# A two-layer attention, expert and recurrent kernel on one core: one chain for the experts' sum, a new order on every engine, and the last sums on TensorE

## The chip, the core and the metric

The kernel runs on one core of a Trainium2 chip. The metric is the device time of one execution in microseconds; the slowest core counts, and here there is one.

## What is computed

The input x has 128 sequences of 64 rows and 128 features, that is 8192 rows or 64 tiles of 128 rows; the context has the same shape. Four blocks follow each other, each with a residual:

```python
x = x + L0_xattn(layernorm(x), ctx, ctx)   # 16 heads of 8, biases, 64 queries against 64 keys of the same sequence
x = x + L0_ffn(layernorm(x))               # 8 experts, the two best by a gate
x = x + L1_xattn(layernorm(x), ctx, ctx)   # 16 heads, no biases
x = x + L1_ffn(layernorm(x))               # a recurrence over the 128 sequences

# the experts: every expert is computed, w is zero for those not chosen
scores = xf @ W_gate + b_gate
w = one_hot(top_k(scores, 2)) weighted by the two scores
out = sum_e w[:, e] * (relu(xf @ W1[e] + b1[e]) @ W2[e] + b2[e])

# the recurrence: one cell state of (64, 128), 128 steps, its end added to every row
ft = sigmoid(xt @ wf.T + c @ uf.T + bf); it = sigmoid(...); gt = tanh(...)
c = ft * c + it * gt
h = tanh(x @ wo.T + c_final @ uo.T + bo)
```

The last line needs the final state, so nothing of the output can be finished before the last of the 128 steps.

## The kernel before

All of x and ctx stays in SBUF (tiles `x` and `cx`, 64 tiles of 128 x 128). A software pipeline written out in full runs over iterations i from FIRST to LAST. In iteration j of the normalisation the four blocks work on different tiles: the first on tile j, the experts on tile j - L1, the second attention on tile j - L2, the recurrence on tile j - L3. Each small step is a Python function, and the table `LAG` says how many iterations after its tile's turn a step stands. Each engine's loop calls its functions in a fixed order, written by hand; engines meet through semaphores (`sig(name)`), one for each step, and wait for counts. With L3 = 10 there are 74 turns of x, 54 of which carry all four blocks; the others, at both ends, carry fewer.

PSUM has seven banks in rotation (`banks[0:7]`) and one, `lstm`, for the recurrence. `USES` lists the 23 uses of an iteration in TensorE's order, and who reads each. A use takes the next bank, so TensorE waits until the reader of the use seven places ahead is done (function `bank`). The readers S0 to S3 of the scores are VectorE's differences D0 to D3.

What the steps are called in the profile:

- `x` to `xn` (L596, ScalarE) is the normalisation; it needs `rs` and `mr` (L1076, L1078, GpSimd), which need VectorE's `mv`, `nm`, `ve` (L813 to L817, function `spread`). `xn` is turned by TensorE (L301) and copied to `xT` by ScalarE (L583, once an iteration).
- Scores (L334), their maxima `mx` (L827, VectorE, four an iteration) and differences to `Ex` (L841, four), exponentials (L625, ScalarE), turns (L349) and copies `ET` (L636), values (L379), halves of the row sums `h` (L1092 and L1096, GpSimd, two pairs an iteration), sums `sm` (L852) and reciprocals (L863), `aT` (L875), the projection (L395), its addition to x (L888).
- The experts: `sc`, `top`, `tix`, `tif` (L899 to L920), the two weights `wa` and `wb` (L931), their sum `we` (L943), its bf16 pieces `wep` (L1123 to L1129, GpSimd), hidden layers (L418), outputs y0 and y1 in two banks (L439), and in `combine` eight SCALAR_TENSOR_TENSOR (L961), which add the weighted outputs in two chains: `acc0` starts from x, `acc1` from the experts' bias, which ScalarE copied from PSUM (L699). L965 adds the two chains into x.
- The recurrence: products (L486), gates (L717 to L719, ScalarE), then `AB` (L975) and `CG` (L978, VectorE), twice an iteration (functions `update(i, 0)` and `update(i, 1)`); two SBUF inputs each.
- `Km` (L1049) and `Vb` (L1063), GpSimd, spread keys and values; L1106 adds the bias of the first attention to x.

```python
                        e.scalar_tensor_tensor(d, b[:, 128 * n:128 * n + 128], we[:, s, k:k + 1],
                                               d if n or c else x[:, t, :], ALU.mult, ALU.add).then_inc(sig(f"acc{c}"), 1)
```

At the end `cU` (L1030) is the last state's part of the output, and `finish` adds it to `cx`, which by now holds x @ wo.T, in chunks of 512 columns (L1166), ScalarE takes the tanh (L765), and the same engine adds the chunk to x (L1172) for SP to store. `TAIL` gives 44 tiles to VectorE and 20 to GpSimd.

Of the kernel before, what the change touches and what calls it, by code (L numbers as in the profile page):

```python
# [7 lines left out]
P = 128  # L8
NT = 64
# [27 lines left out]
L1, L2, L3 = 4, 6, 10  # L37
LAG = {"kv": 0, "sB": 2, "S": 1, "xin": 1, "h0": 1, "h1": 1, "e0": 2, "pv": 3, "sA": 1, "rt": 3,
# [7 lines left out]
OFF = (0, L1, L2, L3)  # L46
FIRST, LAST = -1, NT + 12
# [6 lines left out]
USES = [("kv", "kvc", 0, "C", 1), ("S0", "D0", 1, "A", 1), ("S1", "D1", 1, "A", 1),  # L54
# [10 lines left out]
def on(t):  # L65
    return 0 <= t < NT


def build(nc, a, const, out):
    ctx = ExitStack()  # L70
    with ctx:
# [70 lines left out]
        acc = sb("acc", [P, 2, 2, 128])  # L142
# [36 lines left out]
        def sync_program(e):  # L179
# [42 lines left out]
            lo, done = 0, {"dve": 0, "pool": 0}  # L222
            for adder, n in TAIL:
                done[adder] += 1
                e.wait_ge(sig("out_" + adder), done[adder])
                e.dma_start(o_v[:, lo:lo + n, :], x[:, lo:lo + n, :]).then_inc(sig("stored"), 16)
                lo += n
# [4 lines left out]
        def tensor_program(e):  # L232
            def bank(i, name, done=()):
# [258 lines left out]
            for i in range(FIRST, LAST):  # L492
                if i == FIRST + 1:
                    project_bias()
                if FIRST + 2 <= i < FIRST + 5:
                    turn_weights(i - FIRST - 1)
                keys_values(i)
                step(i, 1)
                scores(i)
                cell_inputs(i)  # L500
                hidden(i, 0)
                hidden(i, 1)
                turn_e(i, 0)
                values(i)
                step(i, 0)
                turn_r(i)
                turn_x(i)
# [728 lines left out]
```

## Time and profile before

| | |
|---|---|
| median of 3 runs | 980.34 us (980.33 to 986.9) |
| profiled execution | 981.66 us, of which the span of the trace is 979.7 |
| busy share of the span | TensorE 88%, VectorE 86%, ScalarE 84%, GpSimd 63% |
| TensorE's granted clock, mean | 0.964 |
| chain that ended last | VectorE 60%, TensorE 20%, no visible cause 12%, ScalarE 3% |

Busy times are means over ramps and steady iterations, so a time for one iteration is better read from two starts of the same instruction, one iteration apart. The spans of neighbouring instructions overlap by some 0.08 us: what an instruction takes from its engine is the distance from its start to the next start, not its own length.

### The profile page before, as it was taken

What the parts mean: (1) busy time and instruction counts of PE and PEld (TensorE: products, weight loads), DVE (VectorE), ACT (ScalarE), POOL (GpSimd) and SP (SyncE); (2) the same over time, 40 slices, a digit from 0 to 9 for tenths busy, and PEclk for the clock granted to TensorE, in tenths of its full rate; (3) what the DMA queues carried; (4) which work ended last, traced back from release to release, by engine and by line L of the source; (5) the groups of instructions that cost most, each with busy time, mean ns of one, the idle gap of its engine ahead of it and who ended that gap; (6) DMA issues with size and microseconds to landing.
All of it is one profiled execution on the core that took longest, in us unless ns stands there. A gap on an engine that the chain in (4) does not pass through costs nothing.

```text
span 979.7 us, 37648 instructions
## 1 busy us (share of the span) xinstructions
PE 859.3 (88%) x13267; PEld 763.5 (78%) x13267; DVE 843.1 (86%) x2878; ACT 820.0 (84%) x2650; POOL 618.8 (63%) x1026
## 2 busy tenths in 40 slices
PE   2778889999999999999999999999999999988750
PEld 1467778888888888888888888888888888877540
DVE  0377899999999999999999999999999999988638
ACT  2467789999999999999999999999999999877633
POOL 2455666676766676766676766676766676754415
PEclk9689999999999999999999999999999999999975
DMA  6920000000000000000000000000000000000006
GB/s 134 250 58 2 2 3 3 3 4 3 2 3 3 3 3 3 3 3 3 3 3 3 2 3 3 3 3 3 3 3 2 4 3 3 3 2 2 2 1 171
DMA packets 37991, 17.34 MB, mean 18 GB/s; under 512 B 9176, under 2 KB 37792, under 8 KB 37808
## 3 DMA queue, kind: packets, MB, share of 16 engines
q1 hardware_dynamic: 37248, 14.67, 5.9%
q8 instruction: 110, 1.80, 0.8%
q14 instruction: 73, 0.60, 0.2%
q0 software_dynamic: 128, 0.07, 0.1%
q10 hardware_dynamic: 432, 0.21, 0.1%
HBM read 10.74 MB, written 4.19 MB: 15 GB/s over the span
## 4 chain that ended last, share of the span: by engine, by line
DVE 60%; PE 20%; issue 12%; ACT 3%; SPq 2%; DVEq 1%; POOL 1%; DMA 0%; ACTq 0%; POOLq 0%
DVE acc L961 13%; DVE mx L827 11%; DVE Ex L841 11%; PE ps L395 4%; PE ps L349 3%; DVE x L965 3%; PE ps L360 3%; PE ps L301 3%; DVE AB L975 3%; DVE x L888 2%; DVE mv L813 2%; PE ps L439 2%; DVE st L786 2%; DVE CG L978 2%; PE ps L461 2%
## 5 line engine op out<-in xcount | busy, mean ns | idle before, releaser
L1092 POOL TENSOR_TENSOR h<-Ex 128x512 f32<-128x512 f32 (+1 forms) x140 | 165.6, 1183 | 155.0 <-issue 135.8
L827 DVE TENSOR_REDUCE mx<-ps 128x8 f32<-128x512 f32 (+1 forms) x280 | 166.1, 635 | 30.5 <-PE ps L334 30.5
L636 ACT ACTIVATE ET<-ps 128x512 f32<-128x512 f32 (+1 forms) x280 | 160.5, 573 | 10.3 <-PE ps L349 10.0
L841 DVE TENSOR_TENSOR Ex<-ps,mx 128x512 f32<-128x512 f32 (+1 forms) x280 | 165.6, 630 | 0.0
L349 PE MATMUL ps<-cst,Ex 128*128 128x128 f32 x1024 | 150.1, 276 | 4.8 <-ACT kv L564 2.1
L625 ACT ACTIVATE Ex<-Ex 128x512 f32<-128x512 f32 (+1 forms) x280 | 152.5, 611 | 0.0
L1076 POOL TENSOR_TENSOR rs<-ve,half 128x4 f32<-128x4 f32 (+3 forms) x74 | 69.1, 934 | 119.9 <-DVE ve L817 119.9
L677 ACT ACTIVATE hT<-ps,col 128x128 f32<-128x128 f32 x512 | 137.2, 371 | 0.0
L439 PE MATMUL ps<-w,hT 128*128 128x128 f32 x1024 | 131.6, 283 | 0.0
L349 PEld LDWEIGHTS ps<-cst,Ex 128*128 128x128 f32 x1024 | 119.3, 143 | 9.6 <-ACT kv L564 4.4
L418 PE MATMUL ps<-xT,w 128*128 128x128 f32 x1024 | 125.4, 276 | 0.0
L439 PEld LDWEIGHTS ps<-w,hT 128*128 128x128 f32 x1024 | 122.5, 196 | 0.0
L418 PEld LDWEIGHTS ps<-xT,w 128*128 128x128 f32 x1024 | 119.5, 192 | 2.3 <-issue 2.3
L961 DVE SCALAR_TENSOR_TENSOR acc<-ps,we,acc 128x128 f32<-128x128 f32 x448 | 121.1, 342 | 0.1
L596 ACT ACTIVATE xn<-x,mr,rs 128x128 f32<-128x128 f32 x256 | 106.1, 484 | 9.9 <-POOL mr L1078 9.5
L1096 POOL TENSOR_TENSOR h<-h 128x256 f32<-128x256 f32 (+1 forms) x140 | 96.3, 688 | 20.2 <-POOL h L1092 0.5
L379 PE MATMUL ps<-ET,Vb 128*32 128x64 f32 x4096 | 72.5, 222 | 25.7 <-DVE Ex L841 25.5
L379 PEld LDWEIGHTS ps<-ET,Vb 128*32 128x32 f32 x4096 | 61.1, 111 | 42.3 <-DVE Ex L841 41.9
L717 ACT ACTIVATE TG<-ps,col 128x64 f32<-128x64 f32 x128 | 39.5, 309 | 52.5 <-PE ps L486 52.5
L334 PE MATMUL ps<-Km,qT 32*64 32x256 f32 x2048 | 74.5, 394 | 7.1 <-DVE acc L961 7.0
L1049 POOL TENSOR_TENSOR Km<-kT,cst 128x512 f32<-128x512 f32 x64 | 66.5, 1040 | 21.4 <-ACT kT L554 21.4
L486 PE MATMUL ps<-CG,wT 128*64 128x64 f32 x1536 | 71.5, 230 | 3.3 <-DVE CG L978 3.3
(111 smaller groups left out, 1951.2 us busy)
## 6 DMA issues: line engine op xcount, KB each, us to landing
out_dram<-x SPq DMA_DIRECT2D x15, 256.0 KB, 2.5
x<-in_x_dram SPq DMA_DIRECT2D x7, 512.0 KB, 7.0
cx<-in_ctx_dram SPq DMA_DIRECT2D x7, 512.0 KB, 6.8
w<-in_L_ffn_W_dram SPq DMA_DIRECT2D x2, 512.0 KB, 5.1
x<-in_x_dram SPq DMA_DIRECT2D x1, 256.0 KB, 3.0
cx<-in_ctx_dram SPq DMA_DIRECT2D x1, 256.0 KB, 3.3
out_dram<-x SPq DMA_DIRECT2D x2, 128.0 KB, 2.2
b<-in_L_ffn_b_dram SPq DMA_DIRECT2D x9, 4.0 KB
```

The source lines that it names most:

```text
L349: m = e.transpose(b[:, 128 * n:128 * n + 128], Ex[:, j % 2, r, 128 * n:128 * n + 128], ident)
L379: m = e.matmul(b[32 * r:32 * r + 32, 128 * c + 64 * n:128 * c + 64 * n + 64], Vb[:, c, j % 4, n, r, 2 * w:2 * w + 2, :].rearrange("p a c - ...
L418: m = e.matmul(b[:, 128 * n:128 * n + 128], w1[:, 4 * c + n, :], xT[:, (t + L1) % 2, 1, :], start=True, stop=True, skip_group_check=True)
L439: m = e.matmul(b[:, 128 * n:128 * n + 128], hT[:, t % 2, 4 * c + n, :], w2[:, 4 * c + n, :], start=True, stop=True, skip_group_check=True)
L596: m = e.activation(xn[:, s, k, :], x[:, j - OFF[k], :], ACT.Identity, bias=mr[:, s, k:k + 1], scale=rs[:, s, k:k + 1])
L625: e.activation(Er, Er, ACT.Exp, scale=SCALE).then_inc(sig(f"E{r}"), 1)
L636: e.activation(ET[:, j % 2, r, lo:hi, :, :], b[:, 256 * lo:256 * hi].rearrange("p (c w q) -> p c w q", c=hi - lo, w=2), ACT.Copy).then_inc ...
L677: m = e.activation(hT[:, t % 2, k, :], b[:, 128 * n:128 * n + 128], ACT.Relu, bias=col[:, B1 + k:B1 + k + 1])
L827: e.tensor_reduce(mx[:, j % 2, r, 4 * lo:4 * hi], b[:, 256 * lo:256 * hi].rearrange("p (j k) -> p j k", k=64), AX.X, ALU.max).then_inc(sig ...
L841: e.tensor_tensor(Ex[:, j % 2, r, 256 * lo:256 * hi].rearrange("p (j k) -> p j k", k=64), b[:, 256 * lo:256 * hi].rearrange("p (j k) -> p ...
L961: e.scalar_tensor_tensor(d, b[:, 128 * n:128 * n + 128], we[:, s, k:k + 1], d if n or c else x[:, t, :], ALU.mult, ALU.add).then_inc(sig(f ...
L1092: e.tensor_tensor(u, v[:, :, :, 0:32], v[:, :, :, 32:64], ALU.add).then_inc(sig("half1"), 1)
```

## The change

The experts' sum becomes one chain: `combine(i, 0)` adds the bias bank to x (no copy by ScalarE), and `combine(i, 1)` to `combine(i, 8)` add the eight weighted outputs one after the other into one `acc`, the last one into x. The nine steps are called apart, so that others stand between some of them. `gate_sum` moves to GpSimd. All engines get a new order, `LAG` and `USES` are new, L1, L2, L3 are 5, 9, 14, and the loop has 81 iterations in place of 77, with 78 turns of x, 50 of them full. The turns of the later weights stand 4 iterations later. In the tail GpSimd has no part: for 30 tiles TensorE adds cU to cx by two products with the identity into a bank, from which ScalarE takes the tanh; for 34 tiles VectorE adds as before; VectorE alone adds the results to x.

```diff
-TAIL = [("dve", 4), ("pool", 4), ("dve", 4), ("dve", 4), ("pool", 4), ("dve", 4),
...
+TAIL = [("dve", 4), ("pe", 4)] * 7 + [("dve", 4), ("pe", 2), ("dve", 2)]
+EARLY = 2
-L1, L2, L3 = 4, 6, 10
+L1, L2, L3 = 5, 9, 14
-FIRST, LAST = -1, NT + 12
+FIRST, LAST = 0, NT + 17
...
-                if FIRST + 2 <= i < FIRST + 5:
-                    turn_weights(i - FIRST - 1)
+                if FIRST + 6 <= i < FIRST + 9:
+                    turn_weights(i - FIRST - 5)
...
+            def share(k, part):
+                lo, n = mine[k]
+                src = cx[:, lo:lo + n, :] if part == 0 else cU[:, :].unsqueeze(1).to_broadcast([P, n, 128])
+                return e.matmul(banks[k % 7][:, 0:128 * n], ident, src, start=(part == 0), stop=(part == 1),
+                                skip_group_check=True)
...
+                if n == 0:
+                    b = bank_of("yb", t + L1)
+                    e.wait_ge(sig("yb"), t + 1)
+                    e.tensor_tensor(d, b[:, 0:128], x[:, t, :], ALU.add).then_inc(sig("acc"), 1)
+                    return
+                c, k = (n - 1) // 4, (n - 1) % 4
+                b = bank_of(f"y{c}", t + L1)
+                if k == 0:
+                    e.wait_ge(sig(f"y{c}"), t + 1)
+                    e.wait_ge(sig("we"), t + 1)
+                e.wait_ge(sig("acc"), 8 * t + n)
+                m = e.scalar_tensor_tensor(x[:, t, :] if n == 8 else d, b[:, 128 * k:128 * k + 128],
+                                           we[:, t % 2, n - 1:n], d, ALU.mult, ALU.add)
...
+                e.tensor_tensor(we[:, s, :], wa[:, s, :], wb[:, s, :], ALU.add).then_inc(sig("we"), 1)
```

VectorE before, in a full iteration, from the last of the gate's weights over the experts' sum to the recurrence's second update and the maxima:

```order
L931 SCALAR_TENSOR_TENSOR wb<-cst,tif,top 128x8
L961 SCALAR_TENSOR_TENSOR acc<-ps,we,x 128x128
L961 SCALAR_TENSOR_TENSOR acc<-ps,we,acc 128x128 x7
L965 SCALAR_TENSOR_TENSOR x<-acc 128x128
L794 BN_STATS st<-x 128x6
L863 RECIPROCAL ri<-sm 128x32
L813 BN_AGGR mv<-st 128x2 x4
L816 SCALAR_TENSOR_TENSOR nm<-mv,ones 128x4
L817 SCALAR_TENSOR_TENSOR ve<-mv,ones 128x4
L975 SCALAR_TENSOR_TENSOR AB<-TG,CG 128x128
L978 SCALAR_TENSOR_TENSOR CG<-AB 128x64
L827 TENSOR_REDUCE mx<-ps 128x8 x3
```

VectorE now, from `ve` (which GpSimd waits for) to the same update; L970 is the experts' chain, L981 and L984 are AB and CG:

```order
L833 SCALAR_TENSOR_TENSOR ve<-mv,ones 128x4
L970 SCALAR_TENSOR_TENSOR acc<-ps,we,acc 128x128 x2
L915 TENSOR_TENSOR sc<-ps,bg 128x8
L970 SCALAR_TENSOR_TENSOR acc<-ps,we,acc 128x128
L922 MAX top<-sc 128x8
L970 SCALAR_TENSOR_TENSOR acc<-ps,we,acc 128x128 x2
L929 MAX_INDEX tix<-top,sc 128x8
L970 SCALAR_TENSOR_TENSOR acc<-ps,we,acc 128x128 x2
L970 SCALAR_TENSOR_TENSOR x<-ps,we,acc 128x128
L843 TENSOR_REDUCE mx<-ps 128x8
L981 SCALAR_TENSOR_TENSOR AB<-TG,CG 128x128
L984 SCALAR_TENSOR_TENSOR CG<-AB 128x64
```

Before, the update followed `ve` at once; now the whole experts' chain and one maximum stand between them.

GpSimd before, one iteration from the `rs` that waits for `ve`:

```order
L1076 TENSOR_TENSOR rs<-ve,half 128x4
L1078 TENSOR_TENSOR mr<-nm,rs 128x4
L1092 TENSOR_TENSOR h<-Ex 128x512
L1096 TENSOR_TENSOR h<-h 128x256
L1063 TENSOR_TENSOR Vb<-kv,cst 128x8x16 x2
L1123 CAST wep<-we 128x24
```

GpSimd now, from the same `rs`:

```order
L1106 TENSOR_TENSOR rs<-ve,half 128x4
L1108 TENSOR_TENSOR mr<-nm,rs 128x4
L1093 TENSOR_TENSOR Vb<-kv,cst 128x8x16 x2
L1164 CAST wep<-we 128x24
L1166 TENSOR_TENSOR wer<-we,wep 128x8
L1168 CAST wep<-wer 128x24
L1170 TENSOR_TENSOR wep<-wer,wep 128x24
L1122 TENSOR_TENSOR h<-Ex 128x512
L1126 TENSOR_TENSOR h<-h 128x256
L1122 TENSOR_TENSOR h<-Ex 128x512
L1126 TENSOR_TENSOR h<-h 128x256
```

The values and the gate's pieces now stand ahead of the halves of the sums, and both pairs of halves follow each other.

## Rows read from the trace of the kernel before

**Rows 1.** Stretches: us, busy PE, PEld, DVE, ACT, POOL; clock, DMA share, GB/s.

```profile
0.00:134.30 134.30, 93.13 (x1068) 74.04 (x1069) 79.11 (x282) 80.15 (x258) 69.07 (x126) 0.89 0.34 82
134.30:855.50 721.20, 691.73 (x11155) 628.17 (x11153) 675.96 (x2317) 668.21 (x2147) 494.45 (x811) 1.00 0.01 3
855.50:952.80 97.30, 74.45 (x1050) 61.27 (x1048) 63.76 (x257) 61.85 (x228) 38.83 (x81) 0.94 0.01 2
```

**Rows 2.** Groups by line and form: busy us, mean ns, idle before.

```profile
L583 ACT ACTIVATE xT<-ps 128x512 f32<-128x512 f32 x54 | 32.2, 597 | 3.0
L439 PE MATMUL ps<-w,hT 128*128 128x128 f32 x1024 | 131.6, 283 | 0.0
```

**Rows 3.** Timeline of VectorE, a full iteration: start, length, idle before.

```profile
502.48 0.16 DVE L817 SCALAR_TENSOR_TENSOR ve<-mv,ones 128x4 f32<-128x4 f32 x1
502.55 0.28 DVE L975 SCALAR_TENSOR_TENSOR AB<-TG,CG 128x128 f32<-128x128 f32 x1
502.87 0.23 DVE L978 SCALAR_TENSOR_TENSOR CG<-AB 128x64 f32<-128x64 f32 x1
503.01 1.88 DVE L827 TENSOR_REDUCE mx<-ps 128x8 f32<-128x512 f32 x3
504.81 0.45 DVE L943 SCALAR_TENSOR_TENSOR we<-wa,wb 128x8 f32<-128x8 f32 x1
505.18 1.27 DVE L841 TENSOR_TENSOR Ex<-ps,mx 128x512 f32<-128x512 f32 x2
...
508.66 0.42 DVE L875 TENSOR_TENSOR aT<-ps,rT 128x256 f32<-128x256 f32 x1 [0.41 <-issue]
...
509.59 0.28 DVE L777 BATCH_NORM_STATS2 st<-x 128x6 f32<-128x128 f32 x1
509.95 0.42 DVE L888 TENSOR_TENSOR x<-ps,x 128x256 f32<-128x256 f32 x1
510.29 0.16 DVE L899 TENSOR_TENSOR sc<-ps,bg 128x8 f32<-128x8 f32 x1
...
510.84 0.47 DVE L786 BATCH_NORM_STATS2 st<-x 128x6 f32<-128x128 f32 x2
...
512.05 0.35 DVE L961 SCALAR_TENSOR_TENSOR acc<-ps,we,x 128x128 f32<-128x128 f32 x1
...
514.33 0.47 DVE L965 SCALAR_TENSOR_TENSOR x<-acc 128x128 f32<-128x128 f32 x1
...
515.82 0.16 DVE L817 SCALAR_TENSOR_TENSOR ve<-mv,ones 128x4 f32<-128x4 f32 x1
```

**Rows 4.** Timeline of GpSimd, the same iteration.

```profile
502.71 1.02 POOL L1076 TENSOR_TENSOR rs<-ve,half 128x4 f32<-128x4 f32 x1 [1.41 <-DVE ve L817]
...
503.96 1.27 POOL L1092 TENSOR_TENSOR h<-Ex 128x512 f32<-128x512 f32 x1
505.38 0.73 POOL L1096 TENSOR_TENSOR h<-h 128x256 f32<-128x256 f32 x1
506.07 0.82 POOL L1063 TENSOR_TENSOR Vb<-kv,cst 128x128 f32<-128x128 f32 x2
506.83 0.21 POOL L1123 CAST wep<-we 128x24 bf16<-128x24 f32 x1
...
507.85 1.04 POOL L1049 TENSOR_TENSOR Km<-kv,cst 128x512 f32<-128x512 f32 x1
```

**Rows 5.** Timeline of all engines, in the ramp down.

```profile
884.24 0.48 DVE L931 SCALAR_TENSOR_TENSOR wb<-cst,tif,top 128x8 f32<-128x8 f32 x1
884.24 0.45 POOL L1096 TENSOR_TENSOR h<-h 128x128 f32<-128x128 f32 x1
```

**Rows 6.** Waits, longest in total: us, times, longest.

```profile
PE ps L256 <- DMA wst<-in_L_ffn_ui_dram: 10.8, 1, 10.8
```

**Rows 7.** Timeline of VectorE in the tail.

```profile
952.79 2.36 DVE L1166 TENSOR_TENSOR cx<-cx,cU 128x512 f32<-128x512 f32 x2
...
963.42 0.68 DVE L1166 TENSOR_TENSOR cx<-cx,cU 128x512 f32<-128x512 f32 x1
```

More of the change, by code:

```diff
@@ L221, in sync_program @@
                 load_c(c)
[L222 to L225, printed above, removed]
+            lo = 0
+            for k, (_, n) in enumerate(TAIL):
+                e.wait_ge(sig("out"), k + 1)
                 e.dma_start(o_v[:, lo:lo + n, :], x[:, lo:lo + n, :]).then_inc(sig("stored"), 16)
@@ L237, in bank @@
                 while v >= len(USES) * FIRST:
-                    _, reader, lag, chain, times = USES[v % len(USES)]
+                    _, reader, lag, chain, step, first = USES[v % len(USES)]
                     n = v // len(USES) - lag - SPAN[chain][0]
@@ L241, in bank @@
                         if reader not in done:
-                            e.wait_ge(sig(reader), times * (n + 1))
+                            e.wait_ge(sig(reader), step * n + first)
                         break
@@ L494, in tensor_program @@
                     project_bias()
-                if FIRST + 2 <= i < FIRST + 5:
-                    turn_weights(i - FIRST - 1)
+                if FIRST + 6 <= i < FIRST + 9:
+                    turn_weights(i - FIRST - 5)
+                hidden(i, 0)
                 keys_values(i)
+                step(i, 0)
+                values(i)
+                query(i)
+                turn_e(i, 3)
+                turn_w(i)
+                turn_e(i, 1)
+                turn_x(i)
+                out_inputs(i)
+                project(i)
+                expert_bias(i)
+                experts(i, 0)
+                turn_e(i, 2)
+                turn_r(i)
+                gate(i)
+                ctx_turn(i)
+                experts(i, 1)
+                turn_e(i, 0)
                 step(i, 1)
                 scores(i)
+                hidden(i, 1)
                 cell_inputs(i)
[L501 to L507, printed above, removed]
-                turn_e(i, 2)
-                turn_w(i)
-                out_inputs(i)
-                project(i)
-                gate(i)
-                expert_bias(i)
-                experts(i, 1)
-                experts(i, 0)
-                ctx_turn(i)
-                query(i)
-                turn_e(i, 3)
-                turn_e(i, 1)
+            mine, lo = [], 0
+            for adder, n in TAIL:
+                if adder == "pe":
+                    mine.append((lo, n))
+                lo += n
+            def share(k, part):
[3 more added lines that the diff above has]
+                                skip_group_check=True)
+            for _, reader, _, chain, step, first in USES:
+                e.wait_ge(sig(reader), step * (SPAN[chain][1] - 1) + first)
+            for k in range(EARLY):
+                share(k, 0)
             e.wait_ge(sig("C"), 2 * NT + 1)
@@ L1030, in vector_program, with share @@
             e.tensor_tensor(cU[:, :], lstm[:, 384:512], bo1[:, :], ALU.add).then_inc(sig("cU"), 1)
-            finish(e, "dve")
+            e.wait_ge(sig("cU"), 1)
+            e.wait_ge(sig("xo"), NT)
+            lo = [sum(n for _, n in TAIL[:k]) for k in range(len(TAIL) + 1)]
+            mine = [k for k, (adder, _) in enumerate(TAIL) if adder == "dve"]
+            def share(k):
+                e.tensor_tensor(cx[:, lo[k]:lo[k + 1], :], cx[:, lo[k]:lo[k + 1], :],
+                                cU[:, :].unsqueeze(1).to_broadcast([P, lo[k + 1] - lo[k], 128]),
+                                ALU.add).then_inc(sig("pre_dve"), 1)
+            share(mine.pop(0))
+            share(mine.pop(0))
+            for k in range(len(TAIL)):
+                e.wait_ge(sig("tanh"), k + 1)
+                e.tensor_tensor(x[:, lo[k]:lo[k + 1], :], cx[:, lo[k]:lo[k + 1], :], x[:, lo[k]:lo[k + 1], :],
+                                ALU.add).then_inc(sig("out"), 1)
+                if mine and k % 2 == 0:
+                    share(mine.pop(0))
         def gpsimd_program(e):
```

187 lines of the change are left out of this document (79 added, 108 removed), and 29 rows, old and new, of tables (LAG, USES).

## The prediction

> **What bounds the kernel now.** I read the table of stretches first [rows 1]. The kernel has three parts: 134.3 us until the recurrence joins, 721.2 us in which the 54 turns of x with all four blocks run [rows 2], so 13.36 us each, and 97.3 us down to the last state; a tail of 26.9 us follows, from 952.8 to the end of the span at 979.7. In the full turns TensorE is busy 691.7 of 721.2 us, VectorE 676.0 and ScalarE 668.2: no engine can be 10% slower, and none alone is full. The chain of waits decides between them: 60% of it is VectorE. So I walked one iteration of VectorE, from `ve` to `ve`, 502.48 to 515.82, 13.34 us [rows 3]. Its only wait of note is 0.41 us ahead of `aT`. What a faster VectorE can give is the question, and TensorE's 691.7 / 54 = 12.8 us is near: its matmul ends are modelled and its waits inside are short, so I put its own limit at 12.6 to 12.8 us an iteration.
>
> **VectorE's work in a full iteration**, in starts to next starts [rows 3]:
> - out: `we` (L943), 504.81 to 505.18, 0.37, now GpSimd's;
> - out: the old sum. Eight L961 take 512.05 to 514.33, 2.28: seven at 0.26 and 0.46 for the last, whose successor waits for two results of VectorE itself. L965 takes its 0.47 and about 0.04 until its reader starts. Together 2.79;
> - out: `sc` to `tix` as a chain of small ones that wait for each other, 510.29 to 510.84, 0.55; in the new order they stand between members of the experts' chain and fill its gaps;
> - out, if the new order does what it can: the wait at `aT` (two differences at 0.60 from 506.98 would let it start at 508.18, it starts at 508.66, so 0.48), and 0.16 at 509.59, where the statistic needs 0.20 and x comes after 0.36;
> - in: nine steps of one chain. A step that waits for the one just ahead starts 0.03 after its end (AB is 0.28 long from 502.55, CG starts at 502.87), so 0.35 + 0.03 = 0.38 in place of 0.26. Steps 1 to 2, 2 to 3, 3 to 4, 6 to 7 and 7 to 8 cost 0.38 each: 1.90 (`sc` and `top` hide in two of them). Step 4 to 5 crosses to the other bank and has three waits: 0.46 like the last L961. Step 5 to 6 holds the index search: 0.26 + 0.15 = 0.41. The last is free of followers: 0.26. The first, with the bias, is half of L888's work: 0.21. Together 3.24;
> - in: `stats_attention` now follows the addition to x directly and waits for it, 0.12.
>
> 13.34 - 0.37 - 2.79 - 0.55 - 0.64 + 3.24 + 0.12 = 12.35 us. So the moved and merged work is worth about 0.35 us (0.37 + 2.79 + 0.55 - 3.24 - 0.12), the better order up to 0.64.
>
> ScalarE loses the bias copy, 0.16 us of its 12.4; GpSimd gains a 128 x 8 sum, 0.2 us on 494.5 / 54 = 9.2. Neither becomes the bound.
>
> **What the order brings in: the port.** L943 is a 128 x 8 instruction and yet takes 0.45 us [rows 3]; it ends at 505.26, just after GpSimd's `h` (503.96 + 1.27 = 505.23) [rows 4]. A VectorE instruction with two SBUF inputs does not run beside such a GpSimd instruction, it waits for its end. Two instructions asked at the same time in the ramp down, and GpSimd's goes first: `wb` takes 0.48 us, twice the 0.23 of the larger CG, [rows 5]. In the tail a 128 x 512 addition takes 2.36 / 2 = 1.18 us, and later 0.60 when GpSimd is quiet [rows 7]. The experts' chain reads PSUM and is not touched. AB and CG have two SBUF inputs each. Before, they stood behind `ve`, when GpSimd computed `rs`, and took 0.28 and 0.23.
>
> Now count both engines from the start of `ve`, the common point. GpSimd: `rs` starts at 0.23, the work behind it at 1.48 (503.96 - 502.48); two Vb take 0.76, the four pieces 1.02, so `h` (L1122) runs from 3.26 to 4.53 and the second half from 4.68 to 5.41 [rows 4]. VectorE: 0.07 + 1.90 + 0.46 + 0.41 + 0.26 + one maximum 0.60 = 3.70: AB asks in the middle of `h`. It gets in when `h` is done and ends at about 4.68; CG asks at 4.71, when the second half has just begun, and ends at 5.41 + 0.08 = 5.49. Undisturbed it would end at 3.70 + 0.32 + 0.23 = 4.25. That is 1.24 us an iteration, on VectorE's own stream, where nothing covers it: the next maximum and all four differences stand behind it, and behind those TensorE's banks for the values, the query and the turns. The distance from `ve` to AB holds no wait for a slower engine as far as I can find one (TensorE's y0, y1 and S0 would each be there 0.5 us or more early), so it repeats. It would have to be off by 0.9 us to either side to go away.
>
> 12.35 + 1.24 = 13.59 us an iteration. The bounds: 12.6 (no stall, TensorE's limit) and 13.9 (both updates, below).
>
> **The ramps.** Before, 54 of 74 turns were full; now 50 of 78. Work is only moved: VectorE's busy time up to the last state was 79.1 + 676.0 + 63.8 = 818.9 [rows 1]. It loses about 64 x 0.72 = 46 us of busy time (L943 and most of L965) and gains some 5 for three more turns in which the attention runs by halves: 778. The 50 full turns hold 50 x 11.8 = 590 of it, which leaves 188 for the ramps against 142.9. Before, ramps took 134.3 + 97.3, less the 10.8 us in which TensorE stood at the turn of the weights until the last of them had landed [rows 6], so 220.8, a fill of 0.65. The 10.8 us go: four iterations later all weights are there. At 0.65 the ramps take 290 us, at 0.72, with the looser lags, 261, at 0.60 313. I take 0.67, near the row: 280. The weights' turns themselves are the same work.
>
> **The tail.** VectorE now has 17 additions to x and 9 of cU with GpSimd quiet: 23 at 0.60 and 3 of half size at 0.34, 14.8 us. TensorE: one product of 128 columns costs 131.6 / 512 = 0.257 us (two records each) [rows 2], so 30 tiles twice are 15.4, less 2.0 done early, at the full clock. The ramp down has a granted clock of 0.94 [rows 1], and it falls towards its end, when the recurrence alone runs; at 1.2 GHz throughout, TensorE would need 27 us. With about 2.2 us before the first result and 2.5 for the last store I take 19.5 us against 26.9; bounds 18 and 30.
>
> **The sum.** 280 + 50 x 13.59 + 19.5 = 979 us of span, against 979.7. The profiled execution lies 1.9 above its span and 1.3 above the median of the runs, so 979.6: I forecast **980 us**. A measurement of this kernel can tell about 1% from no change. In terms: full turns 679.5 against 721.2, ramps 280 against 231.6, tail 19.5 against 26.9.
>
> **Rivals.**
> 1. CG wins the port. CG asks only 0.03 us after GpSimd's second half starts. If it came first, only AB waits, 0.70 us: 13.05 an iteration, 27 us less, 953. Against it: GpSimd won a tie [rows 5].
> 2. No stall: the chain is short or AB finds the port free, and TensorE's 12.75 is the bound: 280 + 637.5 + 19.5, 938 us. The chain would have to be cheap: with steps at 0.26 AB asks 0.8 us earlier, ahead of `h`. For it: nothing in the rows; the pair AB, CG speaks against. The Trainium skill, VectorE: DVE Perf Modes, section "The DRAIN you can't avoid", has it that the semaphore between VectorE instructions costs nothing extra. By that the single chain is as cheap as two, and this rival would be the forecast; the trace disagrees, 0.26 from start to start in alternation against 0.32 for the shorter AB with its reader behind it.
> 3. Slower: the other update is caught too. `gate_sum` starts on GpSimd when `wb` ends, and the addition of the bias to x (0.46 us) follows it; CG of `update(i, 0)` asks about 0.49 us after the start of `wb`, the addition starts at about 0.46. If GpSimd is first, CG waits 0.28 more: 13.87 an iteration, 994 us. It decides from 0.03 us. Ramps at a fill of 0.60 would add 33 to any case and end on the same side.
> 4. The tail gives nothing, since TensorE stays at 1.2 GHz: 990 us.
>
> **Chances.** The forecast (AB and CG of one update wait) 0.40, rival 1 0.15, rival 2 0.19, rival 3 0.24, rival 4 0.02. With the ramps' uncertainty the forecast is within 1% of the 980.3 in 0.29 of its 0.40, rival 3 slower by more in 0.19, rivals 1 and 2 are faster. Faster 0.40, same 0.35, slower 0.25. The range that leaves out no more than 2 in 10 goes from 942 (most of rival 2 left out) to 998.
>
> **What the profile after would show.** A constant distance of 13.5 to 13.7 us between two `ve`; L981 with a mean well over 0.28 and L984 over 0.23, in one of the two updates each; L970 with starts 0.38 apart; L256 without a wait for a DMA; ramps of 280 us together; tail additions at 0.60. Wrong I would be if L981 shows 0.28 throughout, or if VectorE shows waits for TensorE between `ve` and AB, which would shift the meeting with `h`.

## The result, and the profile after

The changed kernel takes **939.5 us** (median of 4 runs, 938.75 to 939.64) against 980.68 us (980.33 to 986.9); the ratio is 0.957, with a 95% interval of 0.953 to 0.961. The forecast was 980 us with a range from 942, so the time lies just below the range. The span of the trace is 937.7 us. The same table of stretches as [rows 1], cut where the four blocks run together and where `cU` starts; the columns are span, busy PE, PEld, DVE, ACT, POOL, then clock, DMA share and GB/s:

```profile
0.00:128.90 128.90, 112.10 (x1399) 90.48 (x1400) 104.23 (x381) 102.16 (x343) 90.00 (x173) 0.97 0.36 85
128.90:799.00 670.10, 646.94 (x10337) 579.58 (x10336) 651.23 (x2097) 611.34 (x1946) 472.04 (x801) 1.00 0.01 3
799.00:918.50 119.50, 104.93 (x1540) 85.59 (x1538) 94.42 (x359) 87.36 (x315) 62.37 (x126) 0.96 0.01 2
918.50:937.70 19.20, 11.43 (x28) 5.24 (x28) 15.28 (x27) 9.46 (x17) 0.00 (x0) 0.94 0.77 219
```

In the terms of the prediction:

| | before | forecast | after |
|---|---|---|---|
| full turns | 54 x 13.36 = 721.2 | 50 x 13.59 = 679.5 | 50 x 13.40 = 670.1 |
| ramps, up and down | 134.3 + 97.3 | 280 | 128.9 + 119.5 = 248.4 |
| tail, from `cU` | 26.9 | 19.5 | 19.2 |
| span | 979.7 | 979 | 937.7 |

(The tail of before counts from the end of `cU`; from its start it is 27.2 us, and it is from the start that the others count.) A full turn did not become shorter. There are four fewer of them, and the ramps, now 28 turns of x in place of 20, cost 17 us more than before where 48 more were expected. Of the 41 us that the forecast was too high, 31.6 lie in the ramps, 9.4 in the full turns and 0.3 in the tail.

The timeline of VectorE, one iteration (start, length, idle before), against [rows 3]:

```profile
505.49 0.15 DVE L833 SCALAR_TENSOR_TENSOR ve<-mv,ones 128x4 f32<-128x4 f32 x1
505.56 0.73 DVE L970 SCALAR_TENSOR_TENSOR acc<-ps,we,acc 128x128 f32<-128x128 f32 x2
506.21 0.15 DVE L915 TENSOR_TENSOR sc<-ps,bg 128x8 f32<-128x8 f32 x1
506.32 0.35 DVE L970 SCALAR_TENSOR_TENSOR acc<-ps,we,acc 128x128 f32<-128x128 f32 x1
...
506.71 0.84 DVE L970 SCALAR_TENSOR_TENSOR acc<-ps,we,acc 128x128 f32<-128x128 f32 x2
...
507.61 0.72 DVE L970 SCALAR_TENSOR_TENSOR acc<-ps,we,acc 128x128 f32<-128x128 f32 x2
508.36 0.35 DVE L970 SCALAR_TENSOR_TENSOR x<-ps,we,acc 128x128 f32<-128x128 f32 x1
508.63 0.68 DVE L843 TENSOR_REDUCE mx<-ps 128x8 f32<-128x512 f32 x1
509.23 0.93 DVE L981 SCALAR_TENSOR_TENSOR AB<-TG,CG 128x128 f32<-128x128 f32 x1
510.20 0.77 DVE L984 SCALAR_TENSOR_TENSOR CG<-AB 128x64 f32<-128x64 f32 x1
510.89 0.68 DVE L843 TENSOR_REDUCE mx<-ps 128x8 f32<-128x512 f32 x1
...
516.94 0.28 DVE L981 SCALAR_TENSOR_TENSOR AB<-TG,CG 128x128 f32<-128x128 f32 x1
517.25 0.23 DVE L984 SCALAR_TENSOR_TENSOR CG<-AB 128x64 f32<-128x64 f32 x1
...
518.92 0.16 DVE L833 SCALAR_TENSOR_TENSOR ve<-mv,ones 128x4 f32<-128x4 f32 x1
```

And GpSimd beside it, against [rows 4]:

```profile
505.72 1.02 POOL L1106 TENSOR_TENSOR rs<-ve,half 128x4 f32<-128x4 f32 x1 [1.36 <-DVE ve L833]
...
508.74 1.27 POOL L1122 TENSOR_TENSOR h<-Ex 128x512 f32<-128x512 f32 x1
510.16 0.73 POOL L1126 TENSOR_TENSOR h<-h 128x256 f32<-128x256 f32 x1
...
517.25 0.54 POOL L1136 TENSOR_TENSOR x<-x,bo 128x128 f32<-128x128 f32 x1
```

From `ve` to `ve` it is 13.43 us. The first update lies beside `h` as forecast: AB is asked for 3.74 us after `ve`, takes 0.93 us and ends at 510.16, just after `h` (508.74 + 1.27 = 510.01); CG takes 0.77 beside the second half. The other update, at 516.94, takes 0.28 and 0.23, although its CG starts in the same hundredth of a microsecond as GpSimd's addition of the bias (L1136). The maxima, which read PSUM, take 0.68 beside the same instructions of GpSimd.

### The profile page after: what moved, and what is told of

It reads as the page before. It is cut to its first block and busy times, and to the rows that moved or that the text cites. A ratio compares the mean times of both kernels' runs of the same rounds, so it can differ in the third digit from the quotient of the medians.

```text
span 937.7 us, 37787 instructions
## 1 busy us (share of the span) xinstructions
PE 875.4 (93%) x13299; PEld 760.9 (81%) x13299; DVE 865.1 (92%) x2860; ACT 810.3 (86%) x2617; POOL 624.4 (67%) x1100
## 5 line engine op out<-in xcount | busy, mean ns | idle before, releaser
L349 PE MATMUL ps<-cst,Ex 128*128 128x128 f32 x1024 | 163.7, 279 | 26.3 <-DVE Ex L857 25.9
L843 DVE TENSOR_REDUCE mx<-ps 128x8 f32<-128x512 f32 (+1 forms) x292 | 171.7, 611 | 11.1 <-PE ps L334 11.1
L1122 POOL TENSOR_TENSOR h<-Ex 128x512 f32<-128x512 f32 (+1 forms) x146 | 166.1, 1138 | 14.2 <-POOL h L1126 12.6
L970 DVE SCALAR_TENSOR_TENSOR acc<-ps,we,acc 128x128 f32<-128x128 f32 x448 | 155.5, 347 | 13.3
L649 ACT ACTIVATE Ex<-Ex 128x512 f32<-128x512 f32 (+1 forms) x292 | 167.4, 583 | 0.0
L660 ACT ACTIVATE ET<-ps 128x512 f32<-128x512 f32 (+1 forms) x292 | 150.8, 543 | 18.9 <-PE ps L349 18.3
L349 PEld LDWEIGHTS ps<-cst,Ex 128*128 128x128 f32 x1024 | 115.5, 142 | 38.7 <-DVE Ex L857 37.3
L418 PEld LDWEIGHTS ps<-xT,w 128*128 128x128 f32 x1024 | 123.9, 191 | 25.0 <-issue 24.8
L418 PE MATMUL ps<-xT,w 128*128 128x128 f32 x1024 | 141.1, 282 | 0.0
L439 PE MATMUL ps<-w,hT 128*128 128x128 f32 x1024 | 139.1, 279 | 0.0
L1147 POOL TENSOR_TENSOR we<-wa,wb 128x8 f32<-128x8 f32 x64 | 13.0, 203 | 104.0 <-DVE wb L949 104.0
L981 DVE SCALAR_TENSOR_TENSOR AB<-TG,CG 128x128 f32<-128x128 f32 x128 | 70.7, 552 | 9.4 <-ACT CG L733 9.4
L379 PE MATMUL ps<-ET,Vb 128*32 128x64 f32 x4096 | 72.7, 221 | 3.9 <-DVE Ex L857 3.5
```

Of the source, the lines that this page charges most:

```text
L349: m = e.transpose(b[:, 128 * n:128 * n + 128], Ex[:, j % 2, r, 128 * n:128 * n + 128], ident)
L418: m = e.matmul(b[:, 128 * n:128 * n + 128], w1[:, 4 * c + n, :], xT[:, (t + L1) % 2, 1, :], start=True, stop=True, skip_group_check=True)
L439: m = e.matmul(b[:, 128 * n:128 * n + 128], hT[:, t % 2, 4 * c + n, :], w2[:, 4 * c + n, :], start=True, stop=True, skip_group_check=True)
L649: e.activation(Er, Er, ACT.Exp, scale=SCALE).then_inc(sig(f"E{r}"), 1)
L660: e.activation(ET[:, j % 2, r, lo:hi, :, :], b[:, 256 * lo:256 * hi].rearrange("p (c w q) -> p c w q", c=hi - lo, w=2), ACT.Copy).then_inc ...
L843: e.tensor_reduce(mx[:, j % 2, r, 4 * lo:4 * hi], b[:, 256 * lo:256 * hi].rearrange("p (j k) -> p j k", k=64), AX.X, ALU.max).then_inc(sig ...
```

## The experiments

All times below are medians, and spans are those of the one execution whose trace was taken; the kernel before, run beside them, had 983.2 us in the first group of four, 983.2 in the second, 982.2 in the third and 981.0 beside the last kernel. Times of turns are distances between the copies to `xT`, one a turn.

**ab_early**: the stall taken away, by order alone.

```diff
                 combine(i, 7)
+                update(i, 1)
                 combine(i, 8)
                 maxima(i, 0)
-                update(i, 1)
```

> The changed kernel with one call moved: update(i, 1) stands between combine(i, 7) and combine(i, 8), ahead of the first maximum; nothing else is touched. AB would then be asked for about 2.9 us after the start of ve, 0.4 us before GpSimd's h starts (3.25), and both AB and CG should run in 0.28 and 0.23 us. Theory A (the port stall of 1.2 us on VectorE's own stream sets the 13.44 us between two ve): VectorE falls to about 12.2 us of work, TensorE's 12.8 becomes the bound, the distance between two ve is 12.8 to 13.0 us, the 50 full turns take 640 to 650 us in place of 670, and the whole 910 to 920 us. Theory B (the stall is there but TensorE's own stream already bounds the turn at 13.4): distance 13.3 to 13.45 us, the whole 934 to 940 us, and AB's stall shows up again as a wait of VectorE.

Measured: 895.2 us, ratio 0.910 (0.908 to 0.913), span 892.4. A full turn takes 12.57 us, the 50 of them 628.8. VectorE's timeline, and then GpSimd's:

```profile
509.55 0.29 DVE L981 SCALAR_TENSOR_TENSOR AB<-TG,CG 128x128 f32<-128x128 f32 x1 [0.16 <-ACT CG L733]
509.88 0.22 DVE L984 SCALAR_TENSOR_TENSOR CG<-AB 128x64 f32<-128x64 f32 x1
...
510.28 1.28 DVE L843 TENSOR_REDUCE mx<-ps 128x8 f32<-128x512 f32 x2
```

```profile
509.62 0.31 POOL L1170 TENSOR_TENSOR wep<-wer,wep 128x24 bf16<-128x24 f32 x1
509.89 1.34 POOL L1122 TENSOR_TENSOR h<-Ex 128x512 f32<-128x512 f32 x1
```

GpSimd's `h` now starts at 509.89, when AB is done. The stall was real and on the path: theory A holds, and the gain was larger than its range, mostly because the next bound lies lower (12.57) than the 12.8 taken from TensorE's busy time; the ramp down is also 3.7 us shorter.

**ab_edge**: the same step moved by one place only, behind `combine(i, 8)`.

```diff
                 combine(i, 8)
+                update(i, 1)
                 maxima(i, 0)
-                update(i, 1)
```

> The changed kernel with update(i, 1) moved by one place only: behind combine(i, 8), ahead of the first maximum. AB would be asked for 3.2 us after the start of ve, within 0.05 us of the start of GpSimd's h, and CG in the middle of h. If the port theory holds with both engines' times as read (a stall lasts until the running GpSimd instruction ends): one of the two still waits for the end of h, 0.9 to 1.0 us in place of 1.24, a distance of 13.1 to 13.3 us between two ve, about 922 to 932 us. If what matters is only that AB stands ahead of a maximum: 12.6 us and 895, as in ab_early. If the position makes no difference until AB is ahead of combine(i, 8): 13.44 and 939.

Measured: 934.5 us, ratio 0.951 (0.948 to 0.954), span 932.5; the usual turn is 13.21 us. VectorE's timeline, and then GpSimd's:

```profile
516.88 0.30 DVE L981 SCALAR_TENSOR_TENSOR AB<-TG,CG 128x128 f32<-128x128 f32 x1
517.22 1.18 DVE L984 SCALAR_TENSOR_TENSOR CG<-AB 128x64 f32<-128x64 f32 x1
```

```profile
517.00 1.32 POOL L1122 TENSOR_TENSOR h<-Ex 128x512 f32<-128x512 f32 x1
518.47 0.74 POOL L1126 TENSOR_TENSOR h<-h 128x256 f32<-128x256 f32 x1
```

AB starts 0.12 us ahead of `h` and is undisturbed; CG is asked for 0.2 us after `h` has started, and its 0.23 us become 1.18. The turn came out in the range of the port theory, the whole 2.5 us above it. What decides here is which engine starts first, not the kind of neighbour on VectorE.

**one_product_more**: is TensorE the bound of ab_early?

```diff
-                e.matmul(b[:, 0:128], wT[:, WK, :], cx[:, t, :], start=True, stop=True)
+                for _ in range(2):
+                    e.matmul(b[:, 0:128], wT[:, WK, :], cx[:, t, :], start=True, stop=True)
```

> The kernel of ab_early in which TensorE makes the first product of keys_values(i) twice, into the same place: 0.22 us more of TensorE's work in each of 64 turns, and no other change. Theory A (with the stall gone, TensorE is the bound of the full turn): 12.57 + 0.22 = 12.79 us a turn, 13 to 14 us on the whole, 908 us if ab_early is 895. Theory B (VectorE or a loop sets 12.57): 12.57 to 12.62 a turn, 895 to 898 us.

Measured: 907.5 us, a full turn 12.79 us. The 0.22 us of TensorE's product appear in full, and in ab_early's full turns TensorE is busy 628.4 of 628.9 us: TensorE is the bound. The ramps show more. In the ramp up the turns 5 to 9 took 7.4, 8.0, 8.6, 8.8, 9.0 us in ab_early and take 7.9, 8.3, 8.8, 9.0, 9.3 (in turn 5 the granted clock also fell, from 0.91 to 0.86); the turns 10 to 13 stay at 10.8, 11.0, 11.3, 11.7. The former follow TensorE's work, the latter don't. In the turns 5 to 13 of both kernels the busiest engine is busy for 94% or more of the turn.

**turns_early**: the changed kernel with the weights' turns at the old places.

```diff
-                if FIRST + 6 <= i < FIRST + 9:
-                    turn_weights(i - FIRST - 5)
+                if FIRST + 2 <= i < FIRST + 5:
+                    turn_weights(i - FIRST - 1)
```

(and ScalarE's likewise).

> The changed kernel with the turns of the remaining weights at the places of before (iterations 2 to 4 for TensorE, 3 to 5 for ScalarE). The weights land about 25 us into the span, TensorE would come to them at about 10 us. Theory A (ramps are now set by throughput, so a stop of all engines at the start is paid in full): the second turn of x about 14 us later, the whole 950 to 955 us. Theory B (the short ramps come from the order and the looser lags, and a later start is caught up by blocks that have slack): less than 5 us slower, 940 to 944 us.

Measured: 955.7 us, span 953.8, 16.1 more than the changed kernel. The second turn of x comes at 29.8 us in place of 13.9, the first full one at 145.6 in place of 128.9; full turns and tail are as they were, the ramp down is 0.7 us shorter. A stop at the start is paid in full: theory A, 0.7 us above its range.

**before_late_turns**: the same part, done alone in the kernel before.

```diff
-                if FIRST + 2 <= i < FIRST + 5:
-                    turn_weights(i - FIRST - 1)
+                if FIRST + 6 <= i < FIRST + 9:
+                    turn_weights(i - FIRST - 5)
```

> The kernel before with one part of the change: the remaining weights are turned four iterations later (and the cell's constants three later). The prediction priced this at 10.8 us, the wait of L256 for the last of the weights; in the changed kernel the early places cost 16.7 us. Theory A (only the wait goes): second turn of x 11 us sooner, 970 to 973 us. Theory B (what the wait delays is paid in full by every engine): 966 to 968 us. If it is given back in the next turns, which in this kernel take 13 us whatever work they hold: 976 us or more.

Measured: 970.1 us, ratio 0.987 (0.984 to 0.990), span 968.3, 11.4 less than before; the first full turn comes at 121.6 in place of 134.3. That is theory A. The price of the prediction, 10.8, was nearly right for the old order. The new order comes to that place earlier, and turns_early shows that there the same wait puts the first full turn off by 16.7. (ScalarE's part of the edit moves too, and its scaling of the cell's constants three iterations.)

**before_new_tail**: the new tail alone in the kernel before, with `share` and the final loops of all engines.

```diff
-TAIL = [("dve", 4), ("pool", 4), ("dve", 4), ("dve", 4), ("pool", 4), ("dve", 4),
...
+TAIL = [("dve", 4), ("pe", 4)] * 7 + [("dve", 4), ("pe", 2), ("dve", 2)]
+EARLY = 2
...
-            finish(e, "pool")
```

> The kernel before with the new tail alone: half of the sums of cU by TensorE into PSUM, all additions to x by VectorE, GpSimd quiet. From cU to the end of the span 26.9 us before and 18.9 us in the changed kernel. If the tail's gain is independent of the rest: 972 to 973 us. If TensorE's clock at the end is lower here than in the changed kernel, 974 to 978 us.

Measured: 977.8 us, ratio 0.994 (0.992 to 0.996), span 975.9, 3.8 less than before. From `cU` to the end of the span it is 19.4 us in place of 27.2, but `cU` comes 4 us later. The whole lies in the range that was to mean a lower clock in the tail, but that is not the cause: the granted clock there is 0.85 against 0.94 in the changed kernel, and the tail is as long (19.4 and 19.2). The reason is in TensorE's timeline; here the changed kernel:

```profile
911.35 0.91 PE L486 MATMUL ps<-CG,wT 128*64 128x64 f32 x12 [0.68 <-DVE CG L984]
912.19 0.80 PE L461 MATMUL ps<-wT,xT 128*128 128x128 f32 x2
914.14 3.75 PE L530 MATMUL ps<-cx,cst 128*128 128x512 f32 x4 [1.16 <-issue]
917.82 0.47 PE L539 MATMUL ps<-wT,CG 128*64 128x128 f32 x1
```

The last CG starts at 913.39. The products that turn it into `cU` (L539) are behind the two early sums (L530). By the code these first wait for the last reader of every bank (the profile names no releaser for the 1.16 us ahead of them), and then run 3.75 us at a low clock (905 to 918.5 has a granted clock of 0.62). `cU` follows the last CG by 5.07 us, by 1.03 in the kernel before.

**uo_first**: ab_early with these products first.

```diff
+            e.wait_ge(sig("C"), 2 * NT + 1)
+            c_end = CG[:, (2 * NT) % 3, 0:64]
+            e.matmul(lstm[0:64, 384:512], c_end, wT[:, UO, :], start=True, stop=True, skip_group_check=True)
...
             for _, reader, _, chain, step, first in USES:
                 e.wait_ge(sig(reader), step * (SPAN[chain][1] - 1) + first)
             for k in range(EARLY):
                 share(k, 0)
-            e.wait_ge(sig("C"), 2 * NT + 1)
...
```

> The kernel of ab_early with one more step moved: on TensorE the two products of the last state with UO stand ahead of the two early sums into PSUM (with their waits), not behind them. Theory A (the early sums, 3.75 us at the low clock, run ahead of the products that cU waits for; from the start of the last CG to the start of cU it takes 4.7 us against 1.0 in the kernel before): cU comes 3.5 to 4 us sooner, and as the early sums now lie beside cU and the first additions, the whole is 2.5 to 4 us shorter, about 891 us if ab_early is 895. Theory B (the early sums are needed ahead of the first tanh and their time is only moved behind cU): within 1 us of ab_early.

Measured: 893.2 us (892.4 to 894.6) against ab_early's 895.2 (893.6 to 897.2), ratio 0.909 (0.907 to 0.911), span 892.3 against 892.4. `cU` starts at 869.57, 3.6 us sooner, and VectorE then waits as long for ScalarE, which waits for the first sum from TensorE:

```profile
871.90 0.68 DVE L1050 TENSOR_TENSOR cx<-cx,cU 128x512 f32<-128x512 f32 x1
876.00 1.29 DVE L1058 TENSOR_TENSOR x<-cx,x 128x512 f32<-128x512 f32 x2 [3.42 <-ACT cx L781]
```

In this pair of traces the wait was only moved, as theory B has it. The medians differ by 2.0 us, but the two sets of runs overlap, so that a gain of up to 2 us is neither shown nor excluded.

**tail_two_first**: VectorE makes the first two groups, one early sum.

```diff
-TAIL = [("dve", 4), ("pe", 4)] * 7 + [("dve", 4), ("pe", 2), ("dve", 2)]
-EARLY = 2
+TAIL = [("dve", 4), ("dve", 4)] + [("pe", 4), ("dve", 4)] * 6 + [("pe", 4), ("dve", 2), ("dve", 2)]
+EARLY = 1
```

> The kernel of uo_first with another tail: VectorE makes the first two groups of four tiles alone, TensorE's sums begin with the third group, one early sum in place of two. In uo_first cU came 3.6 us sooner, but VectorE then waited 3.4 us for the first of TensorE's sums. Theory A (the early sum of 1.9 us and its partner of 1.3 are ready by the time that VectorE has done its two groups): that wait goes, one group more on VectorE costs 0.6, 2 to 3 us less than uo_first, about 890 to 891 us beside 893. Theory B (the stores or ScalarE set the end): within 0.7 us of uo_first.

Measured: 892.1 us, ratio 0.908 (0.906 to 0.910), span 890.6. It is the fastest version here, but only just: 1.1 us below uo_first by the medians and 1.7 by the spans, with intervals that overlap. Theory A wanted 2 to 3 us, theory B no more than 0.7, so this run decides for neither. Against ab_early it is 3.1 us by the medians and 1.8 by the spans: of the 4 us, half or more come back.

**before_gate_pool**: one part alone, 0.37 us of VectorE's work moved to GpSimd.

In VectorE's order, and then in GpSimd's:

```diff
-                gate_sum(i)
                 differences(i, 0)
...
+                gate_sum(i)
                 gate_pieces(i)
```

> The kernel before with one part of the change: the gate sum runs on GpSimd, directly ahead of the four pieces, in place of VectorE's L943. Theory A (the full turn of before was bound by VectorE's stream, as the prediction took it): 0.35 us less in each of 54 full turns, about 958 to 962 us. Theory B (the kernel before was held by a loop over several engines, 13.2 us long even in turns with 11.1 us of VectorE's work, and the new order is what opens it): 13.3 us a turn stays, 976 to 981 us.

Measured: 976.3 us, ratio 0.993 (0.991 to 0.995); a full turn 13.27 us in place of 13.34. Of 0.37 us, 0.07 arrive: theory B. (Of the 6.9 us of span, 4.6 are in the full turns and 2.5 in the ramp up, where the granted clock differs too, as told under before_wide.) The chain of waits, one turn of it, says why (start, length, what):

```profile
502.57 0.92 issue x2
503.48 0.43 DVE aT L875
...
504.05 0.68 PE ps L395 x4
...
504.93 1.84 PE ps L439 x16
506.88 0.45 PE ps L314 x4
507.33 0.87 PE ps L349 x8
...
509.23 0.37 PE ps L486 x12
509.84 0.24 ACT TG L718
...
510.71 0.53 ACT rd L649 x2
511.24 0.26 ACT kT L554
...
513.37 0.41 ACT xn L596
...
514.00 1.84 ACT hT L677 x7
```

In the kernel before 60% of the chain was VectorE's. Here VectorE has one step of it, and the rest goes round through TensorE and ScalarE, with a length of 13.27 us. So two loops of nearly the same length seem to have stood side by side; that both exist is tested further down.

**gate_pool_keys_late** took 1.2 us of ScalarE's work out of that second loop by moving `keys_values(i)` behind `relus(i, 1)`.

```diff
-                keys_values(i)
                 scale(i)
                 relus(i, 0)
                 relus(i, 1)
+                keys_values(i)
```

> The kernel of before_gate_pool (the kernel before with the gate sum on GpSimd) with one change of ScalarE's order: keys_values(i) stands behind relus(i, 1), not ahead of scale(i). In before_gate_pool the chain of the full turns ran no longer over VectorE but over xn, hT, aT, the 16 products of the experts, TG, rd, kT, Vb, kv on ScalarE and TensorE, 13.27 us. Theory A (two loops, VectorE's of 13.34 and this one of 13.27, stood side by side in the kernel before, so that neither alone gives anything): with 1.2 us out of the second loop the turn falls to 12.9 to 13.1 us, the whole to 958 to 967. Theory B (the turn is 13.27 for a third reason): no change against before_gate_pool, 974 to 978.

Measured: 1279.0 us, 18.5 us a turn: a miss. The move tied a new and longer loop: its chain goes from hT over kT, Vb, kv and L349 to L379, the turns, the experts, `ve` and `rs` back to xn. By the code the tie is the rotation of the banks: `turn_e(i, 0)` (L349) takes the bank seven uses behind that of `keys_values(i)`, that is the same bank, so TensorE waits there until ScalarE has copied the keys and values, which now come behind `relus(i, 1)`. The run says nothing of the two theories.

**gate_pool_turn_first** and **before_turn_first**: a gentler cut, one swap on ScalarE, with and without the gate sum on GpSimd.

```diff
-                gates(i, 1)
                 turn_e(i, 1)
+                gates(i, 1)
```

> The kernel of before_gate_pool with one swap in ScalarE's order: turn_e(i, 1) stands ahead of gates(i, 1), not behind it, so that the copy (0.48 us) runs in the 0.81 us that ScalarE waits for the recurrence's product. Theory A (the kernel before had two loops side by side, VectorE's of 13.34 us and one through ScalarE and TensorE of 13.27 that holds this wait): with 0.37 us out of the first and 0.48 out of the second, the turn takes 12.9 to 13.1 us, the whole 960 to 970 us in place of 976. Theory B (the second loop goes another way or is a third bound): 13.2 to 13.3 us a turn, 974 to 978.

> The kernel before with that swap alone (turn_e(i, 1) ahead of gates(i, 1) on ScalarE); the gate sum stays on VectorE. Theory A (two loops side by side): VectorE's loop of 13.34 us is untouched, 13.30 to 13.35 us a turn in the full turns and nothing in the whole, 979 to 983 us. Theory B (ScalarE's wait was the bound of the turn all along): 12.9 to 13.0 us a turn, 960 to 965 us.

Measured: 967.1 us (ratio 0.984, 0.982 to 0.986) with both, 13.09 us a turn; 982.5 us (ratio 1.000, 0.998 to 1.001) with the swap alone, 13.34 us a turn. Alone the gate sum is worth 0.7%, the swap nothing, together they are worth 1.6%. That is what two loops side by side do: theory A in both. By the full turns, 13.34 us becomes 13.27 with the gate sum on GpSimd, stays 13.34 with the swap, and becomes 13.09 with both.

**before_wide**: are the shorter turns of the new ramps due to the wider offsets between the blocks, or to the order?

```diff
-L1, L2, L3 = 4, 6, 10
+L1, L2, L3 = 5, 8, 13
...
-FIRST, LAST = -1, NT + 12
+FIRST, LAST = -1, NT + 15
```

> The kernel before with wider offsets between the blocks alone: L1, L2, L3 = 5, 8, 13 in place of 4, 6, 10 (and three iterations more), so 77 turns, 51 of them full; the order on every engine stays. In the kernel before the ten turns ahead of the full ones and the ten behind hold 13.2 and 12.6 us at their longest with 11.1 and 10.4 us of VectorE's work; in the changed kernel they are 97% full. Theory A (the order makes the loops that fix a turn at about 13 us, whatever it holds): turns with three blocks still take 12.3 to 13.5 us, there are more of them, and the whole is 1005 to 1020 us. Theory B (the wider offsets of the changed kernel are what shortened its ramps): turns with three blocks fall to 10.5 to 11.5 us, and the whole stays at 975 to 990 us.

Measured: 994.7 us, ratio 1.012 (1.009 to 1.016), the ramps 167.1 + 124.4 = 291.5 us. Its turns 7 and 8 as stretches:

```profile
88.20:101.40 13.20, 10.60 (x113) 9.16 (x113) 8.73 (x37) 8.44 (x31) 6.91 (x15) 0.87 0.00 1
101.40:114.60 13.20, 10.83 (x129) 9.47 (x130) 10.92 (x37) 8.97 (x34) 6.86 (x15) 0.87 0.01 1
```

13.2 us both, with 8.7 and with 10.9 us of VectorE's work, and no engine above 11. The turns were not shortened to 10.5 to 11.5 us: theory B falls, and in the length of its turns theory A holds. But equal lengths at different fillings do not show that the order fixes the turn whatever it holds, because the granted clock was 0.87 in both. The turn that corresponds to the first of them is turn 5 of the kernel before. Here it is there, and then in before_turn_first, whose swap changes nothing in a turn in which the recurrence does not run yet:

```profile
68.30:81.60 13.30, 10.63 (x113) 9.13 (x113) 8.86 (x37) 8.79 (x35) 7.03 (x16) 0.87 0.01 1
```

```profile
70.40:82.30 11.90, 9.04 (x113) 7.53 (x113) 8.87 (x37) 8.79 (x35) 7.06 (x16) 1.00 0.01 1
```

With the same work, the turn takes 1.4 us less at the full clock. What the old order leaves at the full clock is a gap over the fullest engine: 2.8 us in this turn, 1.3 in turn 7 (12.4 us, 11.1 us of VectorE's work), 1.1 in turn 9 (13.2 us, 12.1). Wider offsets add such turns. The whole came out 10 us below theory A's range: the ramps have six turns more than before (26 against 20) and take 60 us more, 10 each, and three full turns fewer give back 45.

## Why the prediction was wrong

**What bounds the kernel** ("no engine can be 10% slower, and none alone is full. The chain of waits decides between them: 60% of it is VectorE"): half right. By before_gate_pool and its partners VectorE's loop was the longest, by 0.07 us. A second one through ScalarE and TensorE stood right behind it, which a chain of waits can't show, since it shows only the longest. In ab_early the new order runs at TensorE's 12.57 us, below both loops, so this cost nothing in the full turns of the forecast. It cost the ramps, as far as the same loops held them.

**The full turn**, 12.35 + 1.24 = 13.59 forecast, 13.43 measured. The mechanism was right to the tenth: AB asked at 3.74 (3.70), CG ended at 5.48 (5.49), the stall 1.2 us (1.24). The experts' chain from its second step to the first maximum takes 508.63 - 505.56 = 3.07 us (3.03); dependent steps start 0.38 apart, and the step across the banks takes 0.49 (0.46). What was too large is the rest of the walk, from CG's end to `ve`: 7.95 against 8.10 us. The page of the Trainium skill on which rival 2 leaned, "VectorE: DVE Perf Modes", section "The DRAIN you can't avoid", is not borne out by the chain: 0.38 from start to start with a reader behind against 0.26 in alternation [rows 3]. On the port it is the page "SBUF — State Buffer" of the Trainium skill, section "Who interferes with whom", that these runs agree with where VectorE comes second: it makes the shared pair an exclusive lock, and says that issue order decides who blocks; ab_edge shows both within 0.35 us. Where VectorE comes first these runs show less than a full block: GpSimd's instruction becomes longer by some 0.05 to 0.1 us beside an AB or CG of 0.2 to 0.3.

**The ramps** are the step that failed: "Before, ramps took [...] a fill of 0.65 [...] I take 0.67, near the row: 280". They took 248.4 us. VectorE's busy time was nearly as reckoned: 849.9 us up to `cU`, of which some 64 are stalls that count as busy, so 786 against 778. The groups of VectorE in the full turns give them (count, busy us, mean ns):

```profile
L981 DVE SCALAR_TENSOR_TENSOR AB<-TG,CG 128x128 f32<-128x128 f32 x90 | 54.5, 606 | 0.0
L984 DVE SCALAR_TENSOR_TENSOR CG<-AB 128x64 f32<-128x64 f32 x90 | 44.5, 494 | 3.1
```

Undisturbed they take about 285 and 225, so 321 + 269 ns twice a turn, in some 55 turns. The fill was wrong: 198.7 / 248.4 = 0.80, and 0.77 without the 6 us of stalls that fall in the ramps, where I took 0.67. I carried a ratio from the old ramps to the new, as if a ramp's emptiness were a property of ramps. It was in the main a property of the old order. The same stretch of the ramps, before and after, first two of before (turns 6 and 65), then two of after (turns 10 and 67):

```profile
81.60:94.70 13.10, 10.79 (x129) 9.55 (x130) 11.09 (x37) 8.97 (x33) 6.86 (x15) 0.87 0.01 3
867.80:880.30 12.50, 10.94 (x176) 9.69 (x174) 10.40 (x41) 9.24 (x34) 6.89 (x15) 1.00 0.01 3
```

```profile
84.10:94.90 10.80, 9.83 (x135) 8.31 (x135) 10.42 (x39) 8.66 (x32) 7.85 (x18) 1.00 0.02 4
832.90:842.70 9.80, 9.72 (x135) 8.45 (x134) 9.42 (x41) 8.23 (x32) 6.14 (x14) 1.00 0.01 2
```

Before, 1.6 to 2 us of such a turn are empty on the fullest engine; after, one engine is busy for 96% of it or more. TensorE's granted clock is a part of it and not the whole: it is 0.87 in the first row, and the pair of stretches under before_wide shows what that costs a turn of this kind, 1.4 us; but the second row has a gap at 1.00, and so has the turn behind it (12.7 us, fullest engine 10.3). The turns 5, 6 and 8 of the kernel before have this low clock. Turn 8 shows 1.3 us (14.0 against 12.7 in before_turn_first), and with as much for turn 6 the clock's share in the three is at most some 4 us by this estimate. In turns 1 and 2 it counts for nothing: 8.6 and 10.5 us both at 0.55 and 0.50 (before) and at 1.00 (before_turn_first). So in turns with three blocks or more the new order comes close to the throughput of the fullest engine (one_product_more), and the old order did not, even at the full clock. That the old ramp turns are held by the same two loops as the full ones is argued from this and not shown: no chain of waits was cut in a ramp turn alone. The last six turns of the new ramp down are not full either (for example 7.4 us with 6.0 on the fullest engine). From the second turn of x to the first full one, 9 turns before took 102.8 us, 13 after take 115.0. The sign that I could have read was there: at the full clock, turns of the ramp with 2 us less work than a full one, and only 0.6 to 0.8 us shorter.

The start is the smaller part. The second turn of x comes at 13.9 us in place of 31.5. Of these 17.6 us I had credited 10.8, the visible wait; in the new order the same places would cost 16.7 (turns_early), because TensorE comes to them sooner while the weights land at the same time. So of the 31.6 us about 6.8 are the start and some 25 the fuller turns, in which up to 4 may be the clock's.

**The tail**, 19.5 forecast, 19.2 measured from `cU`. But it hid a cost: the early sums, priced as "less 2.0 done early", stand ahead of the products that `cU` needs and delay it by 4 us. The change's tail brought 3.8 us and not 7.7 (before_new_tail); the other 4 stand in the 248.4 us of the ramps.

**The rivals.** Rival 1 fell: CG did not win the port. Rival 3 fell, by luck more than by reckoning: in nearly every turn CG and GpSimd's addition start within 0.01 us of each other, as it had them within 0.03, and VectorE won this tie (CG 0.23, the addition 0.54 in place of 0.46), where GpSimd had won that of [rows 5]. Rival 2 gave 938 us, the time that was measured, and was still wrong: the stall is there in every full turn. Without it and with the real ramps the kernel runs in 895 us, and the period is then TensorE's 12.57 us, just under the 12.6 to 12.8 taken for it. The total fitted because its missing stall (0.7 us a turn) was made up by ramps that were too long. A total that fits does not choose between mechanisms; the distance between two `ve` did.

## What to carry to other kernels

A turn that is 1 us or more longer than the work of its fullest engine, at the full clock, is held by waits between engines, not by work: look at the ramps of a software pipeline for it before you scale anything from them, and expect that another order can shorten the ramps even where the full turns stay. Compare stretches only where the granted clock is the same. A chain of waits names the longest loop only; if a cut there brings a fraction of what it should, read the chain again in the cut kernel, and cut the two together. Where two engines share a port, a few places in the order of one engine can be worth nearly 5% (939.5 against 895.2 us): compare the start of each two-input instruction with what the other engine runs at that time, and put it beside something small.

## What the runs showed of the hardware

- The port works both ways, but not alike. In ab_early GpSimd's small L1170, which meets AB, takes 0.31 us in place of 0.23, and `h`, which meets CG, 1.34 in place of 1.27; VectorE's AB and CG are undisturbed there. Where `h` comes first, VectorE waits for its end.
- The waiting instruction's own length is counted from its request: AB with 0.28 us of work shows 0.93, CG with 0.23 shows 1.18. Busy shares therefore rise with a stall; VectorE at 92% in the changed kernel, 85% without the 64 us of stalls, is no fuller than at 86% before.
- What TensorE needs for a full turn (12.57 us in ab_early, where one more product adds its 0.22 us) lies below its busy time for the same work in the trace of the changed kernel, 646.9 / 50 = 12.9 us.
- The granted clock of the same turn can differ from kernel to kernel: in turn 5 it was 0.87 in the kernel before and 1.00 in before_turn_first, for 10.6 and 9.0 us of TensorE's busy time with the same 113 products.
